# Last stage of a four-layer network: who sets the edge element, and where key-value products, column totals and the scan stand in the order

## The reference

```
qkv = in_proj_weight * x + in_proj_bias          # q, k, v: (n, 65536, 4)
q, k = softplus(q), softplus(k)
s = cumsum(k[:, :, :, None] * v[:, :, None, :], axis=1)
z = cumsum(k, axis=1)
y = einsum('nsi,nsij->nsj', q, s) / einsum('nsi,nsi->ns', q, z)
y = concatenate([ones, y[:, :-1]], axis=1)       # one element later
y = sum(hid_proj_weight * y, axis=-1) + hid_proj_bias    # 4 hidden values
y = sum(out_proj_weight * tanh(y), axis=1) + out_proj_bias
```

## Time and profile before

| | us |
|---|---|
| median of 3 runs | 3220.82 |
| lowest and highest | 3220.05, 3222.2 |
| profiled execution | 3215.99 |
| its span | 3214.2 |
| granted TensorE clock, mean of the span | 0.709 |

### The profile page before, as it was taken

The page is one execution under the profiler, slowest core; times in us unless marked ns, Lnnn a source line. Parts: engine busy times, 40 slices in busy tenths (PEclk is TensorE's granted clock), DMA queues, the critical chain, the costliest instruction groups (busy, mean ns, idle before and its releaser), DMA issues. The chain is left out here.

```text
span 3214.2 us, 31625 instructions
## 1 busy us (share of the span) xinstructions
PE 1549.9 (48%) x11604; PEld 893.3 (28%) x11604; DVE 1985.6 (62%) x1764; ACT 854.6 (27%) x1110; POOL 1777.7 (55%) x1353
## 2 busy tenths in 40 slices
PE   3665551222222222222222220263888888888897
PEld 3454420000100001000110000151454555555555
DVE  4222235555545455555555555575999999999995
ACT  2111151111111111111111100154454454444441
POOL 2000027777777777777777777334544544545542
PEclk8778765555555555555555555586999999999999
DMA  9999863655445554555445553313122212212212
GB/s 371 406 429 429 362 161 118 160 154 142 133 135 150 148 136 132 136 151 147 135 131 138 153 144 104 130 31 95 57 66 92 91 65 93 90 65 100 83 63 92
DMA packets 337893, 483.66 MB, mean 150 GB/s; under 512 B 186016, under 2 KB 277940, under 8 KB 320048
## 3 DMA queue, kind: packets, MB, share of 16 engines
q1 hardware_dynamic: 279120, 330.24, 30.3%
q0 software_dynamic: 58720, 152.72, 16.7%
HBM read 397.28 MB, written 85.45 MB: 150 GB/s over the span
## 5 line engine op out<-in xcount | busy, mean ns | idle before, releaser
L438 POOL DMA_INDIRECT gath<-table,idx x1152 | 1217.0, 1056 | 430.5 <-issue 368.3
L613 DVE TENSOR_TENSOR gath<-gath,p_stat 128x2304 f32<-128x2304 f32 x128 | 327.0, 2554 | 745.9 <-DMA gath<-table,idx 643.5
L650 PE MATMUL p_z<-wz,pairs 128*128 128x384 f32 x384 | 262.2, 814 | 450.6 <-issue 447.3
L496 ACT ACTIVATE zt<-p_z 128x384 f32<-128x384 f32 x192 | 93.4, 492 | 981.2 <-remote 604.7
L650 PEld LDWEIGHTS p_z<-wz,pairs 128*128 128x128 f32 x384 | 98.8, 296 | 602.6 <-issue 591.2
L1269 PE MATMUL p_state<-xt,tri 128*128 128x512 f32 x512 | 239.4, 611 | 41.0 <-DVE prod L1158 40.9
L640 PE MATMUL p_conv<-sides,wconv 128*128 128x512 f32 x64 | 66.3, 1139 | 398.0 <-issue 236.1
L1049 POOL TENSOR_TENSOR gated<-gated,outw 128x512 f32<-128x512 f32 x64 | 124.2, 1946 | 210.0 <-ACT gated L1102 210.0
L1158 DVE TENSOR_TENSOR prod<-p_state,query 128x2048 f32<-128x2048 f32 x80 | 182.2, 2277 | 54.1 <-PE p_state L1274 51.5
L1035 POOL TENSOR_TENSOR query<-query,expo 128x2048 f32<-128x2048 f32 x16 | 72.5, 4534 | 254.3 <-DVE expo L1131 254.3
L658 PE MATMUL p_y<-ident,yt 128*128 128x128 f32 x64 | 17.8, 433 | 389.6 <-DVE yt L621 389.6
(11 more groups left out here) (232 smaller groups left out, 3161.2 us busy)
## 6 DMA issues: line engine op xcount, KB each, us to landing
ring<-in_w SPq DMA_DIRECT2D x64, 2304.0 KB, 19.3
hidw<-in_hidw SPq DMA_DIRECT2D x64, 1024.0 KB, 5.2
table<-zt SPq DMA_DIRECT2D x256, 144.0 KB
table<-zt SPq DMA_DIRECT2D x512, 72.0 KB
gath<-table,idx POOLq DMA_INDIRECT x1152
xt<-in_x SPq DMA_DIRECT2D x4, 1024.0 KB, 8.0
resid<-xt SPq DMA_DIRECT2D x32, 128.0 KB, 2.3
xlate<-resid SPq DMA_DIRECT2D x16, 256.0 KB, 2.8
```

Of the source, the lines that this page charges most:

```text
L438: nc.gpsimd.indirect_dma_start(out=gath[:, t % SLOTS, k].rearrange("p n c -> p (n c)"), out_offset=None, in_=tables[u], in_offset=bass.Ind ...
L613: tt(g, g, w, ALU.mult).then_inc(weighted, 1)
L650: nc.tensor.matmul(p_z[i % ZS][:], pairs[u][:, 4 * J:4 * J + 4].rearrange("p j w -> p (j w)"), wz[:, m * WIDE:(m + 1) * WIDE], start=True, ...
```

## The change

ScalarE, not VectorE, sets the edge element, in a new step `set_edge` after the logarithm of the query and ahead of `take_out`; it gives `y_whole`. ScalarE's `normalise` goes to the front of `main`. On VectorE key-value product 2 and the lost part of the query go ahead of query product 4, key-value product 3 goes behind division 3, and the scan goes from ahead of hidden product 0 to behind the log that is added to the query. On TensorE `output` goes ahead of `state` 4; the column totals are added in three pieces; the first running sum of batch b+1 is split, and its `give` part (`carried`) goes behind `turn`, ahead of `hidden_sum` 2.

```diff
+            def set_edge(b):
+                act.wait_ge(y_ready, b * A + A)
+                last = y[P - LANE:P, :, HALF - 1]
+                nc.scalar.activation(last, last, ACT.Identity, bias=edge[P - LANE:P, 1:2], scale=edge[P - LANE:P, 0:1]).then_inc(y_whole, 1)
...
             def main(b, u, left):          # ScalarE
+                if left == 2:
+                    normalise(b + 2)
                 if left:
                     exponential(key, b + 1, 0)
                     logarithm(b + 1, 0)
                     exponential(query[1 - u], b + 1, 1)
                     logarithm(b + 1, 1)
+                set_edge(b)
                 if not (known(b) and b == 0):
                     take_out(b - 1, b + 1)
-                if left == 2:
-                    normalise(b + 2)
...
                     keys_x_values(b + 1, 1)          # VectorE
+                    keys_x_values(b + 1, 2)
+                    lost_part(b + 1, 1)
                 times_query(b, u, 4)
-                if left:
-                    keys_x_values(b + 1, 2)
-                    keys_x_values(b + 1, 3)
-                    lost_part(b + 1, 1)
                 divide(b, u, 2)
                 divide(b, u, 3)
-                dve.wait_ge(y_ready, b * A + A)
-                nc.vector.tensor_scalar(y[P - LANE:P, :, HALF - 1], y[P - LANE:P, :, HALF - 1], edge[P - LANE:P, 0:1],
-                                        edge[P - LANE:P, 1:2], ALU.mult, ALU.add).then_inc(y_whole, 1)
-                if left:
-                    column_carries(b + 1)
+                if left:
+                    keys_x_values(b + 1, 3)
                 hidden(b, u, 0)
                 hidden(b, u, 1)
                 if left:
                     add_log(query[1 - u], b + 1, 1)
+                    column_carries(b + 1)
                 hidden(b, u, 2)
                 hidden(b, u, 3)
...
                     nc.tensor.matmul(p_state[:, i], tri[:], term(j, i), start=True, stop=False)
+                if n:
+                    carried(b, n)
+
+            def carried(b, n):          # TensorE: what was the second half of state
+                j = (n + A) % TERMS
                 if n == 0:
                     pe.wait_ge(carry_ready, b + 1)
...
                 sum_terms(b, u, 2)          # TensorE
-                state(b, 4)
                 if not (known(b) and b == 0):
                     output(b - 1)
+                state(b, 4)
+                if left:
+                    totals(b + 1, (A, 0, 1))
                 sum_terms(b, u, 3)
+                if left:
+                    totals(b + 1, (2,))
                 sum_terms(b, u, 4)
                 if left:
-                    totals(b + 1, (A, 0, 1, 2, 3)).then_inc(totalled, 1)
+                    state(b + 1, 0)
                 hidden_bias(b, u, 0)
-                if left:
-                    state(b + 1, 0)
                 hidden_sum(b, u, 0)
                 hidden_bias(b, u, 1)
+                if left:
+                    totals(b + 1, (3,)).then_inc(totalled, 1)
                 hidden_sum(b, u, 1)
                 hidden_bias(b, u, 2)
                 if left == 2:
                     turn(b + 2)
+                if left:
+                    carried(b + 1, 0)
                 hidden_sum(b, u, 2)
```

More of the change, by code:

```diff
@@ L1355, in _ @@
             state(0, 0)
+            carried(0, 0)
             turn(1)
```

## The result

The changed kernel took 3176.10 us (median of 4 runs, 3172.39 to 3177.61) against 3221.47 for the kernel before beside it (4 runs, 3220.05 to 3222.2). The ratio is 0.9852, 95% interval 0.9841 to 0.9864: 1.5% faster by the ratio, 45.4 us by the medians. The forecast was 3170 with a range of 3155 to 3190.

The account below looks back on a forecast made before the run. VectorE's own order bounds the kernel (94% busy). Per batch +1.55 −3.62 −1.14, mean −3.34, is −43.4 over thirteen; with −3.6, −4.6 and +0.5 it is −51.1 from 3220.8, said as 3170 us, range 3155 to 3190.

Parts of the forecast that it names:

- B: Rival: the scan is held by GpSimd too, or hidden product 2 is; +1.1 us in 15 batches, 3187 us; chance 0.09.
- D: Rival: TensorE at 1.2 GHz becomes the bound; period 64.1 us, 3284 us in total, slower than before; chance 0.05.
- E: Rival: second `gated` product comes too late to precede hidden product 3, load ready; 1.1 us less per batch, 3153; chance 0.06.
- Key-value product 2, lost part, query product 4: VectorE's new order: query product 4 starts at offset 36.19, state 4 is ready at about 31.8; cost 0.
- Division 3: VectorE newly waits for TensorE's sum 4; division 3 starts at 40.54 instead of 38.99, +1.55 us a batch.
- Edge: VectorE's stretch from division 3 to the scan loses 3.62 us a batch; ScalarE's edge takes 0.3, hidden by key-value product 3.
- Who waits for GpSimd: GpSimd's `take_lost` of the query ends at 40.96, key-value product 3 starts at 41.14: free, by 0.18 us.
- rival C: The stall only moves: `take_lost` still runs and holds key-value product 3; 21 us won, 3200 us; chance 0.07.
- Scan: VectorE's scan fills time before hidden product 2, beside the first `gated` product without being held; −1.14 us a batch.
- Hidden product 3: VectorE's hidden product 3, behind GpSimd's second `gated` product, ends at 56.6; next query product 0 starts at 56.5.
- Normalise: ScalarE's `normalise` at the front is done by 7.7, ahead of the key's abs at 9.13; cost 0 unless DMA is 1.4 late.
- The sum of the stage: Thirteen middle batches −43.4 us, batch 0 −3.6, batch 14 −4.6, batch 15 +0.5; −51.1 in all.

Follow-up runs that it names:

- scan_alone: Kernel before, with only the scan moved behind the log added to the query and TensorE's part needing it behind the turn; 3201.8 us, 0.9941 of before.
- gated_later: Changed kernel, with GpSimd's second `gated` product begun only when hidden product 3 is done; 3051.0 us on the second chip, 0.9807 of before.
- output_norm_back: Changed kernel, with `output` behind `state` 4 and `normalise` behind `take_out` again; 3060.7 us on the second chip, 0.9833 of before.
- short_take: Kernel before, with GpSimd subtracting the query's lost part in only 16 of 512 columns; 3169.0 us, 0.9838 of before.
- edge_back: Changed kernel, with VectorE setting the edge again, between division 3 and key-value product 3; 3071.2 us on the second chip, 0.9873 of before.
- late_lost: Changed kernel, with key-value product 2 and the query's lost part behind query product 4 again; 3104.1 us on the second chip, 0.9981 of before.
- late_lost_totals: late_lost, with the last piece of the column totals ahead of hidden sum 0 on TensorE; 3088.6 us on the second chip, 0.9930 of before.
- edge_alone: Kernel before, with only the edge moved to ScalarE, after the query's logarithm; 3201.1 us, 0.9934 of before.
- after_again: The changed kernel unaltered, timed again on the second chip; 3059.9 us, 0.9843 of the kernel before there.
- after_third: The changed kernel unaltered, timed once more on the second chip beside gated_later; 3061.7 us, 0.9843 of the kernel before there.

## Why the prediction was right, step by step

- **The frame**: what bounds the stage is VectorE's order. Right; the period moved as its timeline did. Of the rivals, B fell by scan_alone, and D did not come: the granted clock was 1.00 in the thirteen batches (0.98 before) and hidden sum 2 took 1.97 us where it had taken 3.36. E did not come by itself, and gated_later shows what it is worth: 0.6 us a batch and not 1.1, since the load then sets hidden product 3 in part.
- **Key-value product 2, lost part, query product 4**: 36.19 forecast, 36.21 in batch 9 (2808.25), without a wait for state 4. Right; `output` is free in both places (output_norm_back).
- **Division 3**: +1.55 forecast, 1.53 in batch 9, 1.49 mean. Right. In batch 0 it was 2.91: there TensorE had been idle for 2.65 us and sum 4 took 3.42, at a granted clock of 0.55, the level of 1.2 GHz.
- **Edge**: −3.62, right, with the reason shown by short_take. ScalarE's instruction took 0.39 us; the 0.3 taken was inside its bounds of 0.29 and 0.80, and it is hidden, except in batch 15: there hidden product 0 starts 1.15 us after division 3 where it was 1.06, the +0.1 of the forecast. The Trainium skill, "ScalarE: Activation LUTs", Rules for kernel authors, prefers VectorE for a multiply or an add by its speed per element. Here edge_back gives the two places a difference of 0.45 us a batch in favour of ScalarE, which had been idle for 3.11 us when it set the edge.
- **Who waits for GpSimd**: 40.96 against 41.14 forecast, in the trace 41.0 (2813.04) against 41.24 (2813.27). Right, by a margin of 0.2 us. What it guards is shown by late_lost and late_lost_totals. How fast the cost of rival C would grow with a start that is only a little late was not tested.
- **Scan**: −1.14, not held; scan_alone gives 1.08. The Trainium skill, "SBUF — State Buffer", Who interferes with whom, says that a VectorE instruction with at most one SBUF input does not contend, unless it runs in a 2-port mode. The scan agrees: 1.22 us with a `gated` product beside it, and 1.22 inside GpSimd's subtraction in edge_alone. The operand count alone does not settle it, though: the edge has one SBUF tensor for input, with two scalars per partition out of SBUF, and was held for 3.2 us. Which of these made it so, no run here tells.
- **Hidden product 3**: ends 56.73 against 56.6. Loads are sometimes later than the hold: in batch 2 hidden product 2 waited 0.48 for its load, in batch 10 hidden product 3 waited 1.50, and these batches took 57.19 and 57.14. That makes about half of the 0.17 us between 56.55 and 56.72; the other eleven batches have a mean of 56.63.
- **Normalise**: 0, with 1.99 us of cover left where 1.4 were counted. Right.
- **The sum of the stage**: −51.1 forecast, −49.5 in the traces (962.3 to 912.8). The thirteen batches gave 41.3 and not 43.4; batch 0 2.1 and not 3.6, where the wait for its slow sum 4 was 1.4 longer than counted (this batch scatters besides: 59.87 and 61.66 in the other two traces of the changed kernel); batch 14 4.9 (61.51 to 56.58; 4.6 forecast, where the 3.34 and half of 1.86 that the prediction gives for it make 4.3); batch 15 gained 1.1 and was to lose 0.5. That last term had the wrong sign. Query product 4 came 2.25 us later, as `output` stood ahead of it (2.7 forecast), but division 3 came at offset 35.34, 35.44 before, and not 0.36 later; output_norm_back has it at 35.43. The rest of the 1.1 us was not in the prediction: hidden product 2 was held less (2.35 instead of 3.19 us), so hidden sum 2 began 0.99 earlier, and it took 1.97 where TensorE had needed 3.49 before. The small error of the whole is partly luck: 3.6 us too much was forecast for batches 0 to 13, and 1.9 too little for the last two.
- **The total**: 6 us above the forecast. 1.6 us of it are the stage's, less than the 3.5 between three traces of the changed kernel; the rest is within the scatter of the stages ahead, whose end differs by 5.6 us between the five traces named under after_again. On the second chip the gain was 51.5 and 47.6 us.

## What to carry to other kernels

A small instruction with a long row need not be slow: look at what another engine was doing when it ended. Where VectorE and GpSimd exclude each other, the price of a long GpSimd instruction is what VectorE has in the queue beside it, so place those VectorE instructions there that read PSUM, and issue GpSimd's work when such a run begins; moving the instruction that shows the wait only passes the wait on. Before two edits are credited apart, run each alone: here 1.16 and 1.08 us made 1.40, and with the reorder 3.17.

## What had not been expected

- The stage with indirect DMAs differs between chips. The 1152 gathers of line 438, the same in every kernel here, had a mean of 1056 to 1060 ns in the six traces of the first chip and of 981 to 984 ns in the seven of the second (1217.0 us busy in the kernel before, 1133.2 in after_third). The medians of these two are alike, 950 and 946 ns, so some of the gathers are slower and not all. The kernel before took 3221.7 and 3111.3 us on the two chips; the gathers' busy time is some 84 us of that difference. A batch of the last stage hardly differs, 56.72 and 56.63 us in the changed kernel.
- A hold of VectorE has a second price: after TensorE's 4.39 us of idle time the next sum ran at 1.2 GHz (a granted clock of 0.55; 3.48 instead of 1.97 us). With the totals piece behind it, this made the 1.2 us a batch between late_lost and late_lost_totals.
